# Three bfloat16 matmuls on constants after pairs 13, 14, 30 and 31 of the second attention

## What is computed

```python
scores = jnp.einsum('bhqd,bhkd->bhqk', Q, K) * scale
u = min(L, max(1, int(np.log(L))))                 # 6 of 512 queries
top_u = jax.lax.top_k(scores.max(axis=-1), u)[1]   # per head
q_sel = jnp.take_along_axis(Q, top_u[..., None], axis=2)
attn = jax.nn.softmax(jnp.einsum('bhud,bhkd->bhuk', q_sel, K) * scale, axis=-1)
ctx = jnp.einsum('bhuk,bhkd->bhud', attn, V)       # put back at rows top_u, else 0
return out @ wo.T + bo
```

## Time and profile before

| | us |
|---|---|
| runs (3) | 1771.38, 1781.53, 1781.59 |
| median | 1781.53 |
| profiled execution, whole | 1781.11 |
| its span from first to last instruction | 1779.1 |

### The profile page before, as it was taken

How to read it: one execution, slowest core, us unless ns; L and a number is a source line. 1 busy time by engine, 2 the same in 40 slices (tenths; PEclk the granted TensorE clock), 3 DMA queues, 4 the chain that set the end, 5 groups by cost and what they waited for, 6 DMA issues and landing times.

```text
span 1779.1 us, 28529 instructions
## 1 busy us (share of the span) xinstructions
PE 1413.6 (79%) x8534; PEld 852.9 (48%) x8534; DVE 1070.3 (60%) x4590; ACT 772.5 (43%) x1903; POOL 814.4 (46%) x1194
## 2 busy tenths in 40 slices
PE   4988788877788799898898899888889988867600
PEld 2544454444677674443444444444434457756600
DVE  3866666767354446776766677777767654533422
ACT  2423232322354466655555455555545455534300
POOL 2254554555432313354445655544554433245576
PEclk9998988989799897978877788888878889988755
DMA  6633401001244430000000000110000113344432
GB/s 173 217 119 114 138 31 54 31 23 40 82 147 144 141 109 17 13 18 19 20 17 24 25 25 19 34 54 16 24 24 13 36 48 125 113 137 142 125 107 70
DMA packets 119768, 125.81 MB, mean 71 GB/s; under 512 B 15552, under 2 KB 109888, under 8 KB 119616
## 3 DMA queue, kind: packets, MB, share of 16 engines
q1 hardware_dynamic: 103232, 90.42, 16.1%
q0 software_dynamic: 16384, 33.59, 6.5%
HBM read 50.15 MB, written 73.79 MB: 70 GB/s over the span
## 4 chain that ended last, share of the span: by engine, by line
PE 55%; DVE 14%; issue 12%; ACT 8%; another core or an unknown queue 4%; POOL 4%; DMA 1%; SPq 1%; ACTq 0%; POOLq 0%; DVEq 0%
PE pair L1774 19%; PE pair L1701 7%; DVE pT L1300 6%; PE bank L1589 4%; PE pair L1712 4%; POOL vmyg L539 3%; PE pair L1565 3%; PE pair L1690 2%; ACT pT L839 2%; ACT apart L723 2%; PE bank L1504 2%; PE bank L1510 1%; PE bank L1538 1%; PE bank L1757 1%
## 5 line engine op out<-in xcount | busy, mean ns | idle before, releaser
L1774 PE MATMUL pair<-kT,apart 32*128 32x512 f32 x2048 | 513.8, 765 | 44.0 <-DVE smax L1300 30.1
L1300 DVE CUSTOM_DVE_ANT_0 pT<-pair,pT 128x256 f32<-128x256 f32 x1024 | 384.9, 418 | 212.2 <-ACT pT L839 147.3
L839 ACT ACTIVATE pT<-pair 128x256 f32<-128x256 f32 x1024 | 333.4, 393 | 303.2 <-PE pair L1774 249.2
L1774 PEld LDWEIGHTS pair<-kT,apart 32*128 32x128 f32 x2048 | 203.2, 218 | 225.0 <-DVE smax L1300 124.0
L1701 PE MATMUL pair<-xeT,unit_w 128*128 128x256 f32 x768 | 196.9, 403 | 0.0
L1196 DVE TENSOR_TENSOR hid<-sg,pair 128x512 f32<-128x512 f32 x96 | 66.0, 687 | 204.7 <-ACT sg L765 177.6
L539 POOL DMA_INDIRECT vmyg<-ybufA,slg x128 | 123.4, 964 | 126.1 <-DVE slg L1216 70.8
L1037 DVE TENSOR_TENSOR pT<-pair,causal 128x512 f32<-128x512 f32 x256 | 158.5, 682 | 30.5 <-PE pair L1565 20.3
L1701 PEld LDWEIGHTS pair<-xeT,unit_w 128*128 128x128 f32 x768 | 149.5, 205 | 18.5
L1712 PE MATMUL pair<-unit_w,hid 128*128 128x128 f32 x768 | 110.3, 290 | 54.4 <-DVE ye L1204 52.3
L485 POOL DMA_INDIRECT dispB<-xnf,sli x128 | 126.7, 990 | 43.7 <-issue 43.7
(11 more groups left out here) (232 smaller groups left out, 2099.5 us busy)
## 6 DMA issues: line engine op xcount, KB each, us to landing
dispB<-zeros SPq DMA_DIRECT2D x16, 1408.0 KB
apart<-dispA SPq DMA_DIRECT2D x96, 128.0 KB
ybufA<-ye SPq DMA_DIRECT2D x48, 256.0 KB
apart<-dispB SPq DMA_DIRECT2D x96, 128.0 KB
ybufB<-ye SPq DMA_DIRECT2D x48, 256.0 KB
dispA<-zeros SPq DMA_DIRECT2D x33, 128.0 KB
xs<-in_x SPq DMA_DIRECT2D x16, 256.0 KB, 3.0
out<-xs SPq DMA_DIRECT2D x16, 256.0 KB
```

The costliest lines, as they stand in the source:

```text
L839: act.activation(rel[n % RING][:, q, :], pair[n % RING][:, q, HALF:SEQ], ACT.Relu).then_inc(s["relu_done"], 1)
L1300: dve.tensor_tensor_reduce(out=rel[n % RING][:, q, :], in0=pair[n % RING][:, q, 0:HALF], in1=rel[n % RING][:, q, :], scale=1.0, scalar=LOW ...
L1774: pe.matmul(pair[n % RING][:, q, :], apart[h][at, j, t * P:(t + 1) * P], kTs[h][at, HALF:], start=True, stop=True).then_inc(s["bsc_done"], 1)
```

## The change

A helper issues three bfloat16 matmuls of constant ones (128 x 128, by 128 x 512) into `bank[0]`. Nothing reads the result. It is called after the score matmuls of pairs 13 and 14 where `last and next` (batches 1 to 14), and of pairs 30 and 31 where `before` and the batch is neither 9 nor 10 (12 batches). That is 14 x 6 + 12 x 6 = 156 matmuls. Because `bank[0]` has other writers and readers, each call first waits: at 13 and 14 for `qm_ready` of the next batch, at 30 and 31 for `rk_done`.

```diff
+            def keep_awake(times):
+
+                for _ in range(times):
+                    pe.matmul(bank[0][:, :].rearrange("p (t n) -> p t n", t=TB), onesb[:, :],
+                              onesb[:, :].unsqueeze(1).to_broadcast([P, TB, P]), start=True, stop=True)
+
...
                     if last and n == 13:
                         select_q(b - 1)
+                    if last and next and n in (13, 14):
+
+                        pe.wait_ge(s["qm_ready"], b + 2)
+                        keep_awake(3)
+                    if before and b not in (MID + 1, MID + 2) and n in (30, 31):
+
+                        pe.wait_ge(s["rk_done"], b + B)
+                        keep_awake(3)
                     if last and n == 15:
                         selected_scores(b - 1, 1 - h)
```

## The result

The changed kernel takes 1823.69 us (median of 4 runs, 1820.34 to 1829.41) beside 1781.56 for the kernel before (4 runs): a ratio of 1.028, with a 95% interval of 1.0241 to 1.0320 (the two medians alone give 1.024). That is 27 us above the forecast of 1797 and 11 above the end of the stated range, 1813. The profiled execution takes 1820.34 us against 1781.11, 39.2 more.

What follows compares the result with a forecast made beforehand. GpSimd's run was taken to bound one leg of each batch, TensorE and VectorE the other. 1781.1 + 19 (pairs 13 and 14) - 3 (pairs 30 and 31) = 1797 us, range 1776 to 1813.

Steps and rivals of the forecast that it cites:

- What bounds the kernel, and the two legs: Second attention, 50.6 us period: GpSimd sets the pace from pair 21 to about next pair 9, then TensorE and VectorE.
- a delay before pair 16 goes into the period: Pairs 13 to 16: TensorE is the one waited for, so starting selected_scores 1.6 us late lengthens the period.
- Price of a call: Each call of three matmuls: 0.75 us of TensorE at full clock, 1.5 at half.
- The full-clock term: Pairs 13 and 14, ten batches at clock 0.95 or more: 1.5 us lost in each, 15 us.
- The half-clock term: Pairs 13 and 14, four low-clock batches: two calls cost 3.0 us, 2.0 comes back; net 1.0 each, 4 us.
- Pairs 30 and 31, -3 us: At 12 batch ends the calls are covered by GpSimd's run and delay the clock's fall somewhat: -0.25 us each.
- Held clock: Rival: the calls hold full clock across the batch ends, saving 40 us, time 1760; chance 0.14.
- Hidden at both places: Rival: ScalarE and VectorE set pairs 13 to 16, so time stays 1781 within 5 us; chance 0.12.
- Lengthened delay: Rival: six more matmuls lengthen the delay of TensorE's results, one us at each of 12 ends, 1812; chance 0.14.
- The signs for it: Expected in the new trace: 0.25 us a matmul, select_q to selected_scores about 4.6 us, period near 52.0, GpSimd's 29.7 unchanged.

Runs made afterwards that it cites:

- hold_9_13_30: The kernel before plus matmuls around pair 9, three behind pair 13, and the change's calls at pairs 30 and 31; 1770.16 us, ratio 0.9973.
- only_30_31: The changed kernel without its calls at pairs 13 and 14; 1762.31 us, ratio 0.9985 to the kernel before.
- before_look: The kernel before, unchanged, run again for a trace on a chip of the other kind; 1544.29 us.
- bridge_end: The kernel before plus six matmuls behind pairs 30 and 31 each, twelve behind pair 0, three behind pair 1; 1757.68 us, ratio 0.9974.

## Why the prediction was wrong

**What bounds the kernel, and the two legs: right.** The leg from `keep` to the last gather did not move in any trace, and the loss is in the other. That a delay before pair 16 goes into the period was right too.

**Price of a call: right.** 0.76 and 0.75 us at full clock, 1.39 at half, for 0.75 and 1.5. Six matmuls against three give the price of each further one: (1.40 - 0.76)/3 = 0.213 us at full clock, (2.68 - 1.39)/3 = 0.43 at half. The Trainium skill ("TensorE: Matmul & The Clock Gate", section "Wait — 56ns, not 53.3ns?") has 215.7 and 426.7 ns; these rows agree.

**The full-clock term, 1.5 us a batch: too small.** The working came to 1.6 and a stretch of 4.57. It was 1.87 and 4.84: a lone pair takes 1.06, the whole time of two, where I put 0.95, and the wait is 0.05 longer. I then rounded 1.6 down to 1.5, with nothing to support it. Twelve batches at full clock make that some 4 us.

**The half-clock term, +1.0 net in each of four batches: this step failed.** I added the two calls, 3.0 us, and let 2.0 come back because "full-row work there should bring the clock back earlier". I left out that the split, too, is paid at half clock: pair 14 or 15 alone takes 2.01 us instead of sharing 2.02. Nothing came back; the whole stretch of 8.27 us passed at 0.50. Measured: 4.8 us more than before in batch 2 (8.27 - 3.43), and 5.4 in batch 6 (8.27 - 2.83), which was at full clock before. The 2.0 had a weak source too. The earlier trace rows shows 6.9 and 7.0 us for batches 2 and 14, but the other two of the four low batches, 5 and 9, took 6.1 and 4.9, so that batch 9 had nothing to give back:

```profile
915.70:921.80 6.10, 6.10 (x20) 0.52 0.00 0
...
1120.10:1125.00 4.90, 4.74 (x21) 0.71 0.00 0
```

How many batches are hit is no constant either (2 and 4 of 14 in two traces of the change, 6 and most of a seventh without pairs 30 and 31). With 12 x 1.9 + 2 x 5 = 33 us in place of 19 the sum would have been 1811. The profiled execution took 1820 and the median 1824. Of the 9 us that are left to 1820, 8 are those outside the stretch; most of them likely come from the calls at pairs 30 and 31, to which the forecast gave -3.

**Pairs 30 and 31, -3 us: right in size when alone** (-0.15%, not told from 0, and 0.50 behind every end), likely wrong beside pairs 13 and 14. Held clock: false on this kind of chip as the kernel stands, true on the other (1.0000 there); forced on this kind it gave 0.9974, and neither is told from nothing. Hidden at both places: false. Lengthened delay: in part true. `keep` to pair 4 took 0.4 to 1.5 us longer with the calls on chips of this kind, and 0.54 points came of it in hold_9_13_30; but only_30_31 lost nothing that can be told, so its price of 12 us in the whole time is not shown.

**The signs for it.** The calls of 0.25 us a matmul, 0.50 behind every end and the same 29.7 us came as written. `select_q` to `selected_scores` was 4.84, not 4.6. The turns of maxima, which stand once in every batch, were to be 52.0 us apart; they run from 699.5 to 1497.5 us, 15 periods of 53.2.

## What to carry to other kernels

Before placing an instruction between two others, ask whether those two ran side by side; on TensorE, matmuls on few rows that share the array lose all of that when something full-row stands between them. Here a pair alone took 1.06 us where two together took 1.07, and at half clock, where that time doubles (2.01 and 2.02), so does the loss. Price every added instruction at both clock levels, and don't let the clock pay it back. A filler pays only in a stretch that sets the pace and that would otherwise run at half clock; before the same filler is kept, its gain must be seen on more than one chip.

## What the runs showed of the hardware that was not expected

**Chips differ by 12 to 13% in this kernel, and not by GpSimd's run.** The same program takes 1544 to 1550 us on two chips and 1759 to 1782 on three or four. Of the 236 us between the traces of before and before_look, 93 lie in the second attention and 85 ahead of it. GpSimd from `keep` to the last gather in before_look:

```profile
769.65 0.23 POOL L503 TENSOR_SCALAR keep<-rank 128x8 f32<-128x8 f32 x1 [3.31 <-DVE rank L1015]
...
798.42 0.94 POOL L539 DMA_INDIRECT vmyg<-ybufA,slg  x1 [0.30 <-issue]
```

29.7 us, as ever. But during the same scatters (they end at 782.4) ScalarE is served several results at a time:

```profile
780.23 1.91 ACT L839 ACTIVATE pT<-pair 128x256 f32<-128x256 f32 x6 [1.75 <-PE pair L1774]
782.29 0.73 ACT L839 ACTIVATE pT<-pair 128x256 f32<-128x256 f32 x2 [0.15 <-PE pair L1774]
```

In the kernel before on the other kind it got one at a time (starts at 886.54, 888.00, 889.45, 890.86 and 893.02) until 893.76. With it goes the leg: 189.8 us over twelve batches instead of 263.3. Why TensorE's results come so much later on one kind than on the other while indirect transfers run, the traces don't say.

**Half-clock time is a poor measure of loss.** The changed kernel and before have the same 283 us of it and differ by 40; bridge_end has 169 and comes to 0.9974, not told from 1.
